# Attention on one Trainium2 core: the scores for the row maxima computed in pairs on the two halves of the TensorE rows

## The reference

```python
Q_sel = jnp.take_along_axis(Q, top_idx[:, :, None], axis=1)
scores = jnp.einsum('bud,bld->bul', Q_sel, K) * scale
attn = jax.nn.softmax(scores, axis=-1)
out_sel = jnp.einsum('bul,bld->bud', attn, V)
```

## Time and profile before

| | us |
|---|---|
| median of 3 runs | 1241.56 (1240.2 to 1243.06) |
| the profiled execution | 1228.09 |
| its span, first to last instruction | 1226.3 |
| mean granted TensorE clock | 0.896 |
| TensorE matmuls busy | 1008.8 (82%) |
| DVE busy | 900.4 (73%) |
| ACT busy | 646.7 (53%) |
| POOL busy | 621.6 (51%) |

### The profile page before, as it was taken

The page is one execution under the profiler, slowest core; times in us unless marked ns, Lnnn a source line. Parts: engine busy times, 40 slices in busy tenths (PEclk is TensorE's granted clock), DMA queues, the critical chain, the costliest instruction groups (busy, mean ns, idle before and its releaser), DMA issues. The chain is left out here.

```text
span 1226.3 us, 29092 instructions
## 1 busy us (share of the span) xinstructions
PE 1008.8 (82%) x7725; PEld 616.7 (50%) x7726; DVE 900.4 (73%) x2189; ACT 646.7 (53%) x1448; POOL 621.6 (51%) x649
## 2 busy tenths in 40 slices
PE   7999002399999999999996776169999999999995
PEld 4444001133333333333333665157778888888884
DVE  4885689788777777777773887937778777777774
ACT  2778196067666666666674453335454444444441
POOL 1688382435554545554436986024554455444543
PEclk9999555589999999989998787579999999999998
DMA  6244771211111111111104895089994232223322
GB/s 222 104 148 153 258 221 60 59 28 37 33 46 31 32 44 33 44 32 32 44 4 130 251 272 172 1 213 216 232 228 79 48 52 43 47 47 52 52 43 27
DMA packets 129163, 118.69 MB, mean 97 GB/s; under 512 B 18064, under 2 KB 117072, under 8 KB 129104
## 3 DMA queue, kind: packets, MB, share of 16 engines
q1 hardware_dynamic: 106840, 95.02, 26.6%
q0 software_dynamic: 20480, 21.53, 11.0%
q10 hardware_dynamic: 1784, 1.44, 0.4%
HBM read 57.27 MB, written 37.60 MB: 77 GB/s over the span
## 5 line engine op out<-in xcount | busy, mean ns | idle before, releaser
L961 DVE TENSOR_REDUCE attend_mxh<-attend_p_a 128x1 f32<-128x512 f32 x416 | 266.3, 686 | 89.3 <-PE attend_p_a L1092 66.5
L1031 ACT ACTIVATE w<-attend_p_b 128x409 f32<-128x409 f32 x480 | 227.5, 514 | 128.3 <-PE attend_p_b L1108 112.4
L1832 ACT ACTIVATE expert_hr<-expert_p,b1t 128x256 f32<-128x256 f32 (+1 forms) x376 | 134.3, 423 | 192.7 <-PE expert_p L1770 138.0
L1725 POOL DMA_INDIRECT out_x<-expert_ys,expert_drop x72 | 122.3, 1699 | 190.7 <-DVE expert_ys L1867 133.5
L1108 PE MATMUL attend_p_b<-attend_qt,w 98*128 98x409 bf16 x480 | 166.9, 352 | 1.6 <-issue 1.3
L1092 PE MATMUL attend_p_a<-w,attend_qt 96*128 96x512 bf16 x384 | 153.4, 403 | 6.7 <-ACT attend_qt L1022 2.2
L905 POOL DMA_INDIRECT attn_d<-outs,idx x93 | 91.0, 978 | 118.9 <-DVE attend_mxh L961 112.5
L1792 PE MATMUL expert_p<-w,expert_hhi 128*128 x800 | 136.7, 273 | 0.6 <-DVE expert_ys L1867 0.2
L1770 PE MATMUL expert_p<-expert_xhi,w 128*128 128x256 f16 x800 | 136.3, 273 | 0.0
L886 POOL DMA_INDIRECT attend_qsel<-q_d,idx x96 | 92.2, 960 | 85.0 <-DVE attend_mxh L961 64.8
L1118 PE MATMUL attend_p_o<-w,attend_vh 128*32 128x409 f32 x1024 | 119.6, 540 | 5.9 <-ACT w L1031 3.1
(11 more groups left out here) (352 smaller groups left out, 1955.9 us busy)
## 6 DMA issues: line engine op xcount, KB each, us to landing
expert_wu<-w SPq DMA_DIRECT2D x88, 256.0 KB
q_d<-project_q SPq DMA_DIRECT2D x32, 256.0 KB
w<-in_L_ffn_w SPq DMA_DIRECT2D x16, 512.0 KB, 4.5
route_wraw<-in_L_ffn_w SPq DMA_DIRECT2D x16, 512.0 KB, 5.0
w<-k_d SPq DMA_DIRECT2D x32, 192.0 KB
k_d<-project_k SPq DMA_DIRECT2D x45, 128.0 KB
x<-in_L_attn_x SPq DMA_DIRECT2D x8, 512.0 KB, 9.6
attn_d<-zero SPq DMA_DIRECT2D x8, 512.0 KB
```

Source lines behind the costliest of these rows:

```text
L961: dve.tensor_reduce(mxh[:, c, k:k + 1], chunk_bank(a)[:, :], AX, ALU.max).then_inc(a_done, 1)
L1031: act.activation(prob[:, j, :], tile_bank(j)[:, 0:TOP], ACT.Exp, scale=SCALE).then_inc(prob_done, 1)
L1725: pool.indirect_dma_start(out=out, out_offset=bass.IndirectOffsetOnAxis(ap=drop[u][:, s:s + 1], axis=0), in_=ys[u][:, s, :], in_offset=Non ...
L1832: last = act.activation(hr[g % 2][:, f, rows], p_1[g][:, f, rows], ACT.Relu, bias=cst["b1t"][:, bass.ds(e[s] * FB + 2 * g + f, 1)], scale= ...
```

## The change

The six products are laid out in another order: the query parts are stored as third, first, first, second, and the stack has eight groups of 16 rows instead of six. The keys of groups 6 and 7 are zero, but for the two rows of ones. A second, smaller key buffer (`kb`) holds every other chunk of 512 keys in rows 64 to 127, with its own order of parts. Each chunk for the maxima now has a contraction of 64 rows and four products (three and a zero group in the upper half) instead of 96 rows and six. Two chunks form a pair: one on array rows 0 to 63 and one on 64 to 127, with tile positions (0, 0) and (64, 0), each into its own bank. Six pairs and the unchanged tail chunk make up the 13. DVE still takes 13 maxima of 512.

The pairs are issued after tiles 1, 3 and 5 (head n+1) and 9, 11 and 13 (head n+2), the tail chunk after tile 7. The bank of the maxima's turn becomes a fourth chunk bank. Pairs 0, 2, 3 and 5 use banks 1 and 2, pairs 1 and 4 use banks 3 and 0, the tail and the turned maxima use bank 3, and the turned queries and tile 0 use bank 0. The turn of the queries makes four groups of 32 rows instead of three. SP issues eight DMAs per head instead of three, 480 KB instead of 384 KB. At the start of the stage DVE fills more, and TensorE waits for `pads_done` ahead of the first pair, so that no unset rows are multiplied.

```diff
-STACK_K = ((0, 3), (3, 2), (5, 1))
-KR = TERMS * HD
+STACK_K = ((0, 0, 1), (1, 0, 2), (3, 0, 1), (4, 2, 1), (5, 1, 1))
+STACK_B = ((4, 0, 1), (5, 0, 1), (7, 1, 1))
+HALF, KR = P // 2, 6 * HD
...
         def chunk_bank(a):
-            return p_a[a % 3] if a < 6 else p_a[(a + 1) % 3]
-
-        q_bank = p_a[2]
+            if a == NA - 1:
+                return p_a[3]
+            return p_a[(3, 0)[a % 2] if a // 2 in (1, 4) else (1, 2)[a % 2]]
+
+        q_bank = p_a[0]
...
+        AHEAD = 3
+        LATER, SOON = (1, 3, 5, 7), (9, 11, 13)
...
                 for u in range(U):
-                    dve.memset(kt[u][KR:KR + 32, :], 1.0)
+                    dve.memset(kt[u][KR:P, :], 0.0).then_inc(zero_done, 1)
+                    dve.memset(kb[u][KR:KR + HD, :, :], 0.0)
+                    dve.wait_ge(zero_done, u + 1)
+                    dve.memset(kt[u][KR:KR + 2, :], 1.0)
...
+                FREED = (-1, 0, 2, 6, 0, 8, 9)
+
+                def scores_pair(n, u, i):
+
+                    if i == 0:
+                        pe.wait_ge(q_done, n + 1)
+                        pe.wait_ge(k_here[u], 16 * (len(STACK_K) + len(STACK_B)) * (n // U + 1))
...
+                    if i == 4:
+                        wait(pe, prob_done, TPB * (n - 1) + 1)
+                        wait(pe, mrow_done, n)
                     else:
+                        wait(pe, a_done, NA * n + FREED[i])
+                    if i < PAIRS:
+                        c, k = divmod(i, NK // 2)
+                        pe.matmul(chunk_bank(2 * i)[:, :], qt[u][0:HALF, c * P:(c + 1) * P], kt[u][0:HALF, 2 * k * CH:(2 * k + 1) * CH],
+                                  start=True, stop=True, tile_position=(0, 0))
+                        last = pe.matmul(chunk_bank(2 * i + 1)[:, :], qt[u][HALF:P, c * P:(c + 1) * P], kb[u][HALF:P, k, :],
+                                         start=True, stop=True, tile_position=(HALF, 0))
...
                 def turn_max(n):
                     pe.wait_ge(v_step, VSTEP * (n + 1))
+                    if has(n + 1):
+                        pe.wait_ge(a_done, NA * (n + 1) + 3)
...
                 turn_q(0, 0)
...
+                pe.wait_ge(pads_done, 1)
+                for i in range(PAIRS + 1):
+                    scores_pair(0, 0, i)
...
                     for j in range(TPB):
                         scores_tile(n, u, j)
-                        if 1 <= j <= 7 and has(n + 1):
-                            bank_of_chunk_free(n + 1, j + 5)
-                            scores_chunk(n + 1, (u + 1) % U, j + 5)
+                        if j in LATER and has(n + 1):
+                            scores_pair(n + 1, (u + 1) % U, AHEAD + LATER.index(j))
```

More of the change, by code:

```diff
@@ L864, in steps, with halves @@
                 run(N - U + c, c)
+        AHEAD = 3
+        LATER, SOON = (1, 3, 5, 7), (9, 11, 13)
+        def halves(i):
+            return range(2 * i, min(2 * i + 2, NA))
         def has(n):
@@ L998, in _ @@
                 minus_maximum(0)
-                for a in range(6):
+                for a in range(2 * AHEAD):
                     maximum(1, a)
@@ L1003, in run @@
                     for j in range(1, 15):
[L1004 to L1007, removed]
+                        if j in LATER and has(n + 1):
+                            for a in halves(AHEAD + LATER.index(j)):
+                                maximum(n + 1, a)
+                        if j in SOON and has(n + 2):
+                            for a in halves(SOON.index(j)):
+                                maximum(n + 2, a)
                         if j == 6 and has(n - 1):
@@ L1060, in turn_q @@
                     pe.wait_ge(tail_here, 16 * (n // U + 1))
+                    wait(pe, a_done, NA * (n - 2) + 10)
+                    GROUPS = (0, 2, 2, 0)
                     for c in range(FULL):
-                        for g in range(TERMS // 2):
-                            pe.matmul(q_bank[32 * g:32 * g + 32, c * P:(c + 1) * P], qsel[u][:, c, g * HD:(g + 2) * HD], cst["identb"][:, :],
+                        for g, of in enumerate(GROUPS):
+                            pe.matmul(q_bank[32 * g:32 * g + 32, c * P:(c + 1) * P], qsel[u][:, c, of * HD:(of + 2) * HD], cst["identb"][:, :],
@@ L1064, in turn_q @@
                                       start=True, stop=True, tile_position=(0, 32 * g))
                     rows = slice(32 * u, 32 * u + QTAIL)
-                    for g in range(TERMS // 2):
-                        last = pe.matmul(q_bank[32 * g:32 * g + 32, FULL * P:TOP], qtail[rows, g * HD:(g + 2) * HD],
+                    for g, of in enumerate(GROUPS):
+                        last = pe.matmul(q_bank[32 * g:32 * g + 32, FULL * P:TOP], qtail[rows, of * HD:(of + 2) * HD],
                                          cst["identb"][rows, rows], start=True, stop=True, tile_position=(32 * u, 32 * g))
```

71 lines of the change are left out of this document (25 added, 46 removed).

## The result

The changed kernel takes 1245.85 us in the median (1238.38 to 1251.97), the kernel before on the same chip 1237.85 (1230.96 to 1243.56): 1.007 of it, 95% interval 1.0053 to 1.0087. Forecast was 0.991. The direction was wrong, and the time lies near the top of the range. The forecast stood on a base of 1241.56 us; 1.007 of that is 1250.2 us, at the range's upper end of 1250.

What follows compares the result with a forecast made beforehand. TensorE was taken as the bound. Heads 1 to 3, 28 and 29 (-3.0 us), heads 0 and 30 (-0.6), the loop (-12.0) and the start (+4.1) made -11.5, taking 1241.56 to 1230 us; range 1221 to 1250.

Steps and rivals of the forecast that it cites:

- Pairs and switches: TensorE's chunk pairs: halves run side by side in 0.22 us, switches 0.09 in and 0.12 back; written-out head -0.60 us.
- A: Rival for the pairs: the halves run one after the other, 0.22 us more per pair; 1267 us, chance 0.10.
- C: Rival for the pairs: a partly shared array makes a pair take 0.28 us; 1239 us, chance 0.12.
- D: Rival for the loop: its lateness shrinks, -0.85 us per loop head; 1222 us, chance 0.12.
- Pair 3, `results` and the DVE's load: Within a head: pair 3's wait for DVE costs nothing; tile 3 to `results` stays 1.36 us, set by ACT.
- Start: Start of the stage: DVE's extra fills, now waited for by TensorE, delay the first maximum by 4.1 us (1.4 to 7.1).
- Loads, "Nothing": SP's queue: eight DMAs per head instead of three and 25% more bytes cost nothing.
- Waits: Pair 1's wait for ACT's copy of the turned queries: covered by 0.2 us, gone where ACT is late.
- Loop: The 24 loop heads: -0.50 us each (bounds 0 and -0.9), -12.0 us together.
- Heads 28 to 30: The last written-out heads: -0.6 us each for 28 and 29, -0.3 for 30.
- Rival B (the clock): Over the loop: time at 1.2 GHz doubles or grows two and a half times; 1242 to 1248 us, chance 0.17.

Runs made afterwards that it cites:

- e1: The changed kernel with the zero fills at the stage's start done by DMAs on ScalarE's queue instead of by VectorE; 1.0089 of the kernel before.
- e7: The kernel before with its own three loads of K plus three into a second K buffer that nobody reads; 1.0101 of the kernel before.
- e4: The kernel before with K loaded by five DMAs instead of three, plus three into a buffer nobody reads; 1.0263 of the kernel before.
- e2: The changed kernel without the three loads per head into the second K buffer after the first four heads; 1.0013 of the kernel before.
- e9: The changed kernel with GpSimd's gathers of the queries left out after the first four heads; 0.9781 of the kernel before.
- e3: The changed kernel with each pair of half-height matmuls replaced by two full matmuls of 96 rows, one after the other; 1.0054 of the kernel before.
- e14: The changed kernel with each head's gathers and scatters exchanged in order on GpSimd, so gathers run beside tiles 9 to 15; 1.0450 of the kernel before.

## Why the prediction was wrong

- **Pairs and switches: right.** From a tile to the pair 0.27 us and from the pair to the next tile 0.32 (0.18 + 0.09 = 0.27 and 0.34 forecast), both halves side by side; rivals A and C are out, and so is D, since the lateness grew. The packing of 3.07 instead of 4 that the Trainium skill gives (TensorE: Matmul & The Clock Gate, Measured speedup vs the span model), on which C leaned, isn't seen here with two halves.
- **Pair 3, `results` and the DVE's load: right.** No wait ahead of pair 3 in heads 1 to 3, and tile 3 to `results` takes 1.37 us (280.39 to 281.76) for the 1.36 forecast.
- **Start: right in size, only half in cause.** 4.9 us for 4.1. The fills end at 240.60 (239.9 worked out from the earlier trace rows), but e1 shows that behind them the copy of the first turn was late in any case: 238.93 here for a turn issued at 232.25, and 235.18 before.
- **Loads, "Nothing": wrong.** I looked at the queue's slack and its bytes, and both have room. The cost is elsewhere: 1.0% for the second buffer's loads and 2.6% for all five extra ones on the kernel before (e7, e4), 0.57% for the second buffer's on the changed one (e2).
- **Waits: this is the step that failed.** "Only 0.2 us of cover is left", I wrote of pair 1, and then took the copy to be as early as in the earlier trace rows; the turn of the maxima's new wait for bank 3 I did not cost at all. With the copy 0.84 us later they are worth 0.55 and 0.53 us in each written-out head (1.95 for 1.40, 1.48 for 0.95), 1.1 us, where the whole gain was 0.60: 12.23 us for 11.03. Both go when the gathers go (1.42 and 1.00 in e9).
- **Loop: -0.50 forecast, +0.56 in the profiled executions.** The medians allow less: of their 8.0 us the start has 4.9, heads 1 to 3 have 1.8 and heads 28 to 30 give 1.3 back, which leaves some +0.1 per loop head, an estimate. Either way the gain is gone. I had the late release in my hands, noted that the trace doesn't tell its cause, and let it stand as a constant. Leaving out what causes it is the largest saving that any of my runs found: without gathers the kernel before is 1.5% faster and the changed one 2.9% (0.9781 / 1.007). My reading is that the change shortened the work between releases and added waits behind them, and so pays more for each; the two waits above show it in the written-out heads, for the loop it is argued.
- **Heads 28 to 30: right within 0.1 us for two** (-0.51 and -0.38 for -0.6 and -0.3), short for head 29 (-0.37 for -0.6). They have no gathers, and there the working holds in the main.
- **Rival B (the clock)** gave the direction, and its 1242 to 1248 is near the time. As a cause it is not the first: from 262 to 297 us it is 1.00, before and after, and heads 1 to 3 still lose 0.6 us each; in e3 it is 0.99 over the loop, and the kernel is still slower than before. In the changed kernel's loop it falls from 0.96 to 0.94: some 12 us more at the lower level, which cost some 6 us, an estimate from the two means.

Open stays what in the chip holds the release. The runs show that it goes with indirect DMAs issued by GpSimd (gathers, and in e14 scatters), that loads of another queue make it worse while gathers run, and that TensorE's later instructions go on being issued meanwhile. Also open is why some places of these DMAs are so much worse than others.

## What to carry to other kernels

When a trace shows a reader waiting 1 us or more for an instruction that was long over, find what causes that before costing anything that adds a wait or a transfer: leave out one kind of DMA at a time, and the head's own time comes out (here 11.6 us for 13.6 in the loop, 11.1 for 12.2 in the written-out heads). A cover of 0.2 us is no cover where releases vary by a microsecond. A DMA's cost is not only its bytes and its queue's slack. And compare a profiled execution with its kernel's median before adding up its heads: here two profiles differ by 21.6 us and the medians by 8.0.

## What the runs showed of the hardware

- Row halves (64 rows each, tile positions 0 and 64) run fully side by side: two streams of 512 columns start within 0.01 us and the next full tile follows 0.32 us after them, against 0.43 from the start of two full matmuls (e3). With the way in, 0.27 against 0.18, it comes to the same.
- ScalarE's copy of the first turn started 1.7 us after the turn's last group of matmuls did in the kernel before (233.48 to 235.18) and 6.7 us in the changed one (232.25 to 238.93), both while GpSimd was issuing gathers; that of the second turn, with none on the way, 0.25 and 0.26 us after it.
- Replacing three indirect gathers per head by plain transfers of the same size took the changed kernel from 1.007 to 0.973 of the kernel before, 3.4%, and the loop's clock from 0.94 to 1.00. The plain ones read neighbouring rows.
- A scatter, also an indirect DMA of GpSimd, goes with a late release too: in e14 a tile is read 1.89 us after its start with scatters alone on the way.
- Splitting three loads into five of the same bytes cost 1.6% (e4 against e7).
